# Graph attention layers: h of two graphs is read back by four DMAs in every second step, and both are split one step on

## The reference

```python
def _L0_gnn_ref(seq_inputs, Wq, bq, Wk, bk, Wv, bv, Wf, bf, graph_mask):
    q = _heads(seq_inputs @ Wq + bq)
    k = _heads(seq_inputs @ Wk + bk)
    v = _heads(seq_inputs @ Wv + bv)
    scores = jnp.einsum('bhqd,bhkd->bhqk', q, k) / np.sqrt(HEAD_SIZE)
    bias = jnp.where(graph_mask, 0.0, NEG)[:, None]
    probs = jax.nn.softmax(scores + bias, axis=-1)
    ctx = jnp.einsum('bhqk,bhkd->bhqd', probs, v)
    ...
    return ctx @ Wf + bf
h = jnp.maximum(_layernorm(x, axis=-1), 0.0)
x = x + _L0_gnn_ref(h, ..., adj)
h = jnp.maximum(_layernorm(x, axis=-1), 0.0)
x = x + _L1_gnn_ref(h, ..., adj)
```

## Time and profile before

| | us |
|---|---|
| median of 3 runs | 1942.06 |
| lowest, highest | 1934.52, 1944.56 |
| the profiled execution | 1940.74 |
| its span on the core | 1938.7 |
| TensorE busy | 1869.9 (96%) |
| VectorE busy | 1479.7 (76%) |
| ACT busy | 1526.5 (79%) |
| POOL busy | 1185.7 (61%) |

### The profile page before, as it was taken

How to read it: one execution, slowest core, us unless ns; L and a number is a source line. 1 busy time by engine, 2 the same in 40 slices (tenths; PEclk the granted TensorE clock), 3 DMA queues, 4 the chain that set the end, 5 groups by cost and what they waited for, 6 DMA issues and landing times.

```text
span 1938.7 us, 58154 instructions
## 1 busy us (share of the span) xinstructions
PE 1869.9 (96%) x15766; PEld 1079.6 (56%) x15766; DVE 1479.7 (76%) x5312; ACT 1526.5 (79%) x4553; POOL 1185.7 (61%) x1800
## 2 busy tenths in 40 slices
PE   3899999999999999999999999999999999999996
PEld 1455555555555555555555555555555555555553
DVE  5788777778777777777777787777787777877765
ACT  3688878878888777888887788888888888888874
POOL 3576666666666566666665666666666666666642
PEclk9999999999999999999999999999999999999999
DMA  6466666666666566666666666666666666655554
GB/s 185 131 188 183 199 179 193 193 189 204 202 183 189 176 190 202 191 184 198 194 205 184 182 192 193 193 199 205 188 192 198 197 204 192 198 182 179 180 168 155
DMA packets 445247, 365.35 MB, mean 188 GB/s; under 512 B 212450, under 2 KB 412132, under 8 KB 444900
## 3 DMA queue, kind: packets, MB, share of 16 engines
q1 hardware_dynamic: 444900, 361.43, 61.9%
HBM read 185.09 MB, written 176.16 MB: 186 GB/s over the span
## 4 chain that ended last, share of the span: by engine, by line
PE 50%; SPq 28%; DMA 9%; issue 8%; ACT 2%; DVE 2%; POOL 1%; POOLq 0%; DVEq 0%; ACTq 0%
SPq L332 21%; PE ps_qk L494 7%; DMA p_dram<-p_blocks 7%; PE ps_shared L494 7%; PE ps_shared L496 7%; PE ps_shared L495 7%; PE ps_qk L496 7%; PE ps_qk L495 7%; PE ps_shared L551 5%; PE ps_scores L571 4%; SPq L324 2%; ACT probs L669 1%; SPq L104 1%; SPq L293 1%; SPq L340 1%
## 5 line engine op out<-in xcount | busy, mean ns | idle before, releaser
L669 ACT ACTIVATE probs<-probs,exp_bias,exp_scale 128x128 f32<-128x128 f32 x1536 | 734.7, 482 | 13.1 <-issue 6.6
L430 POOL TENSOR_TENSOR probs<-probs,row_rcp 128x768 f32<-128x768 f32 x256 | 376.6, 1471 | 545.9 <-DVE row_rcp L831 545.9
L854 DVE CUSTOM_DVE_ANT_0 probs<-ps_scores,mask 128x128 f32<-128x128 f32 x1536 | 345.9, 287 | 40.9 <-issue 40.9
L841 DVE SCALAR_TENSOR_TENSOR qk_lo<-ps_qk,qk_bias,qk_hi 128x512 f16<-128x512 f32 x384 | 279.7, 747 | 112.7 <-ACT qk_hi L653 111.5
L648 ACT ACTIVATE v<-ps_shared 128x384 f32<-128x384 f32 x256 | 125.6, 491 | 259.4 <-PE ps_shared L496 259.3
L864 DVE SCALAR_TENSOR_TENSOR x_tile<-ps_shared,out_scale,x_tile 128x384 f32<-128x384 f32 x256 | 157.6, 616 | 195.5 <-PE ps_shared L496 195.3
L669 ACT ACTIVATION_READ_ACCUMULATOR probs<-probs,exp_bias,exp_scale 128x1 f32 x1536 | 292.2, 190 | 0.0
L653 ACT ACTIVATE qk_hi<-ps_qk,qk_bias 128x512 f16<-128x512 f32 x384 | 259.4, 676 | 38.9 <-PE ps_qk L496 38.9
L437 POOL TENSOR_TENSOR ht_lo<-h_moved,ht_hi 128x384 f16<-128x384 f32 x256 | 236.3, 923 | 53.7 <-ACT ht_hi L639 52.8
L419 POOL TENSOR_TENSOR x_tile<-x_tile,out_bias 128x384 f32<-128x384 f32 x256 | 256.6, 1003 | 0.0
L494 PE MATMUL ps_shared<-wf_hi,ct_hi 128*128 128x384 f16 x768 | 251.7, 328 | 3.8 <-DVE ct_lo L835 3.8
(11 more groups left out here) (85 smaller groups left out, 3544.1 us busy)
## 6 DMA issues: line engine op xcount, KB each, us to landing
p_dram<-p_blocks SPq DMA_DIRECT2D x256, 384.0 KB, 2.4
p_moved<-p_dram SPq DMA_DIRECT2D x1024, 96.0 KB, 2.5
h_dram<-h_blocks SPq DMA_DIRECT2D x256, 192.0 KB, 2.2
h_moved<-h_dram SPq DMA_DIRECT2D x1024, 48.0 KB, 2.0
x_tile<-in_x SPq DMA_DIRECT2D x128, 192.0 KB, 2.8
out_x<-x_tile SPq DMA_DIRECT2D x128, 192.0 KB, 2.3
adj_u<-in_adj SPq DMA_DIRECT2D x64, 64.0 KB, 2.3
wv_raw<-in_L_gnn_Wv SPq DMA_DIRECT2D x2, 576.0 KB, 4.9
```

The source lines that it names most:

```text
L430: nc.gpsimd.tensor_tensor(probs[i % 2][:, :, :], probs[i % 2][:, :, :], row_rcp[i % 2][:, :].rearrange("p (a o) -> p a o", o=1) .to_broadc ...
L669: ins = nc.scalar.activation(probs[i % 2][:, s, :], probs[i % 2][:, s, :], ACT.Exp, bias=exp_bias[i % 2][:, s:s + 1], scale=exp_scale[laye ...
L841: nc.vector.scalar_tensor_tensor(out=qk_lo[b][:, chunk, :], in0=ps_qk[chunk % QK_BANKS][:, :], scalar=qk_bias[layer_of(t)][:, chunk // KT, ...
L854: ins = nc.vector.tensor_tensor_reduce(probs[i % 2][:, s, :], score_bank(i, s // PAIRS)[:, (s % PAIRS) * P:(s % PAIRS + 1) * P], mask[b][: ...
```

## The change

`h_moved` becomes one tile that holds two graphs, side by side. SP still writes h of every graph on its own. But it reads h back only in even steps, for graphs s + 8 and s + 9 together, with four DMAs that each bring both (32 partitions x 8 pieces of 96 numbers), and these stand ahead of the step's reads of probabilities. They wait for the writes of both graphs, the later of which was issued in the same step, and until the pair before has been split. ACT and POOL split both graphs in the odd step that follows: the odd one in the step it had, the even one a step later than before. `h_back` has two semaphores instead of four. The order ahead of the first slot follows suit.

```diff
-        h_moved = [sb(f"h_moved{k}", [P, QUADS, RUN], F32) for k in range(2)]
+        h_moved = sb("h_moved", [P, 2, QUADS, RUN], F32)
...
-        h_back = [sem(f"h_back{i}") for i in range(PER)]
+        h_back = [sem(f"h_back{j}") for j in range(PER // 2)]
...
+            def keep_h(t, i, m):
+
+                wait_apart(sp, count, h_back[i // 2], unit_count(t, m, 16 * QUADS))
+                wait_apart(sp, count, h_blocked, unit_count(t, m, PER, i + 1))
+                sp.dma_start(h_dram[i, :, :, :, :].rearrange("a r b n -> (a r) b n"), h_blocks[i % 2][:, :, :]
+                             ).then_inc(h_kept[i], 16)
+
+            def bring_h(t, i, m):
+
+                wait_apart(sp, count, ht_set, unit_count(t, m, PER, i - 1))
+                for k in (i - 1, i):
+                    wait_apart(sp, count, h_kept[k], unit_count(t, m, 16, 16))
+                for quad in range(QUADS):
+                    sp.dma_start(h_moved[quad * SQ:(quad + 1) * SQ, :, :, :],
+                                 h_dram[i - 1:i + 1, :, :, quad, :].rearrange("g a r n -> r g a n")
+                                 ).then_inc(h_back[i // 2], 16)
...
+                    if exists(hu) and hi % 2:
+                        bring_h(hu, hi, m)
                     if exists(pu):
-                        bring_back(pu, pi, p_dram, p_moved, p_kept, p_back, ctx_summed, m)
-                    if exists(hu):
-                        bring_back(hu, hi, h_dram, h_moved, h_kept, h_back, ht_set, m)
+                        bring_probs(pu, pi, m)
...
-                bring_back(0, i, h_dram, h_moved, h_kept, h_back, ht_set, None)
+                keep_h(0, i, None)
+            bring_h(0, 1, None)
...
             load_weight(1, 3)
-            bring_back(1, 0, h_dram, h_moved, h_kept, h_back, ht_set, None)
             load_weight(1, 2)
...
-                    if exists(hu):
+                    if exists(hu) and hi % 2:
+                        h_lo(hu, hi - 1, m)
                         h_lo(hu, hi, m)
...
-                act.wait_ge(h_back[i], unit_count(t, m, 16 * QUADS, 16 * QUADS))
-                nc.scalar.activation(in_order(ht_hi[b][:, :, rows]), moved_in_order(h_moved[i % 2]), ACT.Copy
+                act.wait_ge(h_back[i // 2], unit_count(t, m, 16 * QUADS, 16 * QUADS))
+                nc.scalar.activation(in_order(ht_hi[b][:, :, rows]), moved_in_order(i % 2), ACT.Copy
                                      ).then_inc(ht_hi_set, 1)
...
-                    if exists(hu):
+                    if exists(hu) and hi % 2:
+                        h_hi(hu, hi - 1, m)
                         h_hi(hu, hi, m)
```

More of the change, by code:

```diff
@@ L267, in build, with moved_in_order @@
         ps_largest, ps_bias = ps_scores[2], ps_scores[3]
-        def moved_in_order(tile):
-            return tile[:, :, :].rearrange("p a (c k) -> p c a k", c=KT)
+        def moved_in_order(k):
+            return h_moved[:, k, :, :].rearrange("p a (c k) -> p c a k", c=KT)
         def in_order(view):
@@ L318, in load_out_bias @@
                 sp.dma_start(f_bias_raw[:, :], layers[l]["bf"].rearrange("(a n) -> a n", a=1)).then_inc(f_loaded, 16)
-            def keep_blocks(t, i, blocked, blocks, dram, kept, back, m):
-                wait_apart(sp, count, back[i], unit_count(t, m, 16 * QUADS))
-                wait_apart(sp, count, blocked, unit_count(t, m, PER, i + 1))
-                sp.dma_start(dram[i, :, :, :, :].rearrange("a r b n -> (a r) b n"), blocks[i % 2][:, :, :]
-                             ).then_inc(kept[i], 16)
@@ L327, in bring_back, with keep_probs @@
-            def bring_back(t, i, dram, moved, kept, back, taken, m):
-                wait_apart(sp, count, taken, unit_count(t, m, PER, i - 1))
-                wait_apart(sp, count, kept[i], unit_count(t, m, 16, 16))
-                for quad in range(QUADS):
-                    sp.dma_start(moved[i % 2][quad * SQ:(quad + 1) * SQ, :, :],
-                                 dram[i, :, :, quad, :].rearrange("a r n -> r a n")).then_inc(back[i], 16)
+            def keep_probs(t, i, m):
+                wait_apart(sp, count, p_back[i], unit_count(t, m, 16 * QUADS))
+                wait_apart(sp, count, p_blocked, unit_count(t, m, PER, i + 1))
+                sp.dma_start(p_dram[i, :, :, :, :].rearrange("a r b n -> (a r) b n"), p_blocks[i % 2][:, :, :]
+                             ).then_inc(p_kept[i], 16)
@@ new lines, in bring_probs @@
+            def bring_probs(t, i, m):
+                wait_apart(sp, count, ctx_summed, unit_count(t, m, PER, i - 1))
+                wait_apart(sp, count, p_kept[i], unit_count(t, m, 16, 16))
+                for quad in range(QUADS):
+                    sp.dma_start(p_moved[i % 2][quad * SQ:(quad + 1) * SQ, :, :],
+                                 p_dram[i, :, :, quad, :].rearrange("a r n -> r a n")).then_inc(p_back[i], 16)
+            def keep_h(t, i, m):
[3 more added lines that the diff above has]
+                             ).then_inc(h_kept[i], 16)
@@ L348, in slot @@
                     if exists(pu):
-                        keep_blocks(pu, pi, p_blocked, p_blocks, p_dram, p_kept, p_back, m)
+                        keep_probs(pu, pi, m)
                     if exists(hu):
-                        keep_blocks(hu, hi, h_blocked, h_blocks, h_dram, h_kept, h_back, m)
+                        keep_h(hu, hi, m)
                     if exists(su) and layer_of(su) == 1:
@@ L373, in _ @@
             for i in range(2):
-                keep_blocks(0, i, h_blocked, h_blocks, h_dram, h_kept, h_back, None)
-            for i in range(2):
-                bring_back(0, i, h_dram, h_moved, h_kept, h_back, ht_set, None)
+                keep_h(0, i, None)
+            bring_h(0, 1, None)
             for i in range(PER):
@@ L379, in _ @@
             for i in range(2, PER):
-                keep_blocks(0, i, h_blocked, h_blocks, h_dram, h_kept, h_back, None)
+                keep_h(0, i, None)
             load_adj(0, None)
-            for i in range(2, PER):
-                bring_back(0, i, h_dram, h_moved, h_kept, h_back, ht_set, None)
+            bring_h(0, 3, None)
             for i in range(PER):
@@ L387, in _ @@
             load_out_bias(1)
-            keep_blocks(1, 0, h_blocked, h_blocks, h_dram, h_kept, h_back, None)
+            keep_h(1, 0, None)
             load_weight(1, 3)
-            bring_back(1, 0, h_dram, h_moved, h_kept, h_back, ht_set, None)
             load_weight(1, 2)
@@ L436, in h_lo @@
                 pool.wait_ge(ht_hi_set, unit_count(t, m, PER, i + 1))
-                nc.gpsimd.tensor_tensor(in_order(ht_lo[b][:, :, rows]), moved_in_order(h_moved[i % 2]),
+                nc.gpsimd.tensor_tensor(in_order(ht_lo[b][:, :, rows]), moved_in_order(i % 2),
                                         in_order(ht_hi[b][:, :, rows]), ALU.subtract).then_inc(ht_set, 1)
```

## The result

The changed kernel took 1926.35 us (median of 14 runs, 1923.43 to 1931.14). The kernel before took 1936.82 us in 14 runs beside them (1929.59 to 1944.56). The ratio is 0.994, with a 95% interval from 0.9927 to 0.9953: 11.6 us faster, between 9 and 14. The profiled execution took 1926.46 us with a span of 1924.3, where that of before had a span of 1938.7. These two lie 14.4 us apart. The profiled execution of before stands 3.9 us above its median, that of after stands on it, so the traces show somewhat more than the median gain.

What follows compares the result with a forecast made beforehand. TensorE and SP's queue were taken to bound the kernel by turns. -13 (p_moved) - 2 (start) + 1 (ACT and VectorE) = -14 us from 1942.06 gave 1928; forecast 1918 to 1932 (0.57), range 1918 to 1943.

Steps and rivals of the forecast that it cites:

- p_moved, -13: TensorE's waits for moved probabilities in steady running: 13 us counted as won, of at most 18.7.
- SP, -2.0 for four issues in the odd step: SP's odd step loses four h reads: 1.73 us of issuing and about 0.3 us of waits.
- The pair read's issue, no addition: SP's even step: four reads of twice the bytes take no longer to issue; the other end was +1.73 us.
- The wait for h's write, +0.5 in an even step: SP's even step: h reads wait for the h write just issued, 0 to 0.5 us, taken as 0.5.
- the fourth rival: SP: issues left out give nothing back, the new wait adds 20 x 0.5 = 10 us; 1950, chance 0.02.
- The odd probabilities land 2.7 us sooner: SP, in the pair shown: next write at 716.7 instead of 719.39, odd probabilities landing 2.7 us sooner.
- Long issues leave a few waits: SP: occasional long issues leave TensorE a few waits, so 13 of the 18.7 us count as won.
- the first rival: SP: the pair read costs what two reads did, p_moved stays late; 1940 us (1934 to 1946), chance 0.25.
- ACT and VectorE, +1: Odd step: the later qk_hi delays VectorE's residual by at most 0.15 us; 1 us in all, for a few pairs.
- waits for ct_lo ahead of v in dozens: TensorE, ahead of the projection of v: a listed sign that the forecast is wrong.
- The third rival: VectorE passes ACT's 0.4 us delay on to the projection of v: +18 us, 1960, chance 0.06.
- The start, -2: First slot: TensorE's 6.39 us wait goes; between nothing and 6.4 us won, taken as 2.

Runs made afterwards that it cites:

- e_three_more_issues: The changed kernel with three small 12 KB reads more issued by SP at the end of every odd step: 1946.65 us, ratio 1.0043.
- e_splits_only: The kernel before with four buffers for h_moved and both splits of a pair in the odd step, SP's order kept: 1939.3 us, ratio 1.002.
- e_order_only: The kernel before, its eight h reads kept, with even steps' reads of h ahead of those of probabilities: 1986.56 us, ratio 1.0255.
- e_pair_behind_probs: The changed kernel with the pair of h read behind the probabilities in the even step: 1924.16 us, ratio 0.9935.
- e_eight_reads: The changed kernel with the pair of h read by eight DMAs of one graph each in the same place: 2018.5 us, ratio 1.0418.
- e_qk_before_splits: The changed kernel with ACT's two splits of an odd step behind that step's last qk_hi: 1924.11 us, ratio 0.993.

## Why the prediction was right, point by point

**The forecast** was 1928 and the measured median is 1926.35. Both its parts are a little off and cancel: the gain is 11.6 where 14 was forecast, and it was counted from the median of three runs, 1942.06, where fourteen give 1936.82. From that, the forecast's -14 would have given 1923. In the profiled executions the sum holds almost to the microsecond (-14 against -14.4).

**p_moved, -13.** Late contexts went from 17.5 to 4.35 us, that is -13.2. The ceiling of 18.7, taken from the rate of matmuls, was good for 17.5. The profiled executions show more than the medians here: the profiled run of before was in the upper half of runs that differ by 15 us, where those of the changed kernel differ by 8. The kernels nearest to the threshold, `e_three_more_issues` and `e_splits_only`, differ most, by 21 and 18 us; that the threshold is why is argued.

**SP, -2.0 for four issues in the odd step.** Confirmed by putting them back: 2.0 us of SP's time for four small reads. The sum of all issues fell by 1.8 us, gaps between them not counted. The rule of the Trainium skill that stood against it ("DMA: Bandwidth & Descriptors", "Anatomy of one DMA") has the fixed cost of a DMA in its completion and not in its setup. That section is headed for the path of GpSimd, so its 50 ns for the dispatch was no price for SP's queue, and the estimate of 0.2 us made from it could not be expected to hold. On SP's queue the setup was not small: SP stood 1.72 us for four reads of 12 KB, and with three or four of them more TensorE was the one to wait. The rule's other half, that the completion is the long part, agrees with the trace: a write of h landed 2.2 us (median) after its issue, and the wait for it alone cost 49 us in `e_order_only`.

**The pair read's issue, no addition.** 1.80 us (median) for four, where the four reads of h of an odd step took 1.74. The rival that it costs what two did, and the one that it costs half, are out. So is "h issues of over 0.6 us each". The step from eight reads to four in the same place was worth 92 us.

**The wait for h's write, +0.5 in an even step.** It measured 0.38 us in `e_order_only` and 0.29 between the two kernels with four more issues. The mechanism of the fourth rival ("the new wait outweighs the issues") is real. I priced it at 20 waits x 0.5 = 10 us, and alone it costs 49, since it puts SP over the threshold in every pair and not just in the twenty that waited already. That step of the working was wrong by a factor of five, without harm to the forecast: with the issues gone SP is under 14.36 and the wait is free, as `e_pair_behind_probs` shows.

**"The odd probabilities land 2.7 us sooner."** This step failed in size. The sum of two steps had given 1.5 us and only the pair written out gave 2.7, since its even step was taken 0.6 us shorter instead of 0.5 longer. From the landing of the odd probabilities to the start of the context that uses them there are 0.79 us now (median), and there were 0.50. Two things take the rest. SP ran into VectorE, as its late start fell from 1.80 to 1.04 us and in even steps to 0.09. And the odd step's write of probabilities lands 2.91 us after its issue (median), where it took 2.37: in flight ahead of it are now four reads of probabilities, 384 KB, directly behind the 384 KB of the pair read, where before the last ones ahead of it were 192 KB of h. The two are seen together; that the bytes are the cause is argued, not shown. Their number alone does not set it: `e_eight_reads` has the same bytes in the same order ahead of this write, and there it landed after 2.56 us. The 0.3 us sufficed all the same: contexts with at most 0.12 us to spare went from 36 to 7. The even ones gave 6.88 - 5.21 = 1.7 us of slack, where I had said 2.5.

**Long issues leave a few waits.** Issues of over 0.9 us number 98 after and 112 before, so one falls into most pairs. They moved: before, 77 of them fell on reads of h, and now 4 do, but 69 on reads of probabilities (26 before). On the pair read in this place, where the first rival wanted them, they hardly fell. I had summed SP's need for two steps to 12.9 without one and 14.1 with one. The issues put back place it at 13.0 on average, worked out from a kernel in which SP ends last. The mean between the writes of the changed kernel itself, 14.46, is TensorE's pace and says only that SP is not over it.

**ACT and VectorE, +1.** ACT behaves as said: its wait ahead of v in odd steps is 0.24 us (mean) where it was 0.62, and 0.65 in the earlier trace rows. VectorE in the changed kernel, an odd step, answers to the earlier trace rows:

```profile
712.68 1.63 DVE L857 SCALAR_TENSOR_TENSOR qk_lo<-ps_qk,qk_bias,qk_hi 128x512 f16<-128x512 f32 x2
714.23 0.97 DVE L823 STREAM_TRANSPOSE p_blocks<-probs 128x768 f32<-128x768 f32 x1
715.24 0.62 DVE L880 SCALAR_TENSOR_TENSOR x_tile<-ps_shared,out_scale,x_tile 128x384 f32<-128x384 f32 x1
```

The idle 0.27 us ahead of the residual has gone (0.05 on average), as the delay was to use it up. The projection of v starts late for 10.9 us in all, where it was 8.5: +2.4, of the order of the +1. The splits are not shown to be the cause of it, as `e_splits_only` has both in the odd step and 8.5 us, and `e_qk_before_splits` has 11.6. The sign of being wrong, "waits for ct_lo ahead of v in dozens", was badly chosen. The list of waits names 7 of them, but by the starts of the weight loads all 43 late projections are waits for it, and so were 35 in the kernel before: they were there all along, and most belong to VectorE's wait for the mask. The pair of the earlier trace rows is one of them. The third rival, 18 us slower, did not come about, and the splits alone are within 0.5% of nothing.

**POOL, 0.** It has both splits in a piece of 1.79 us and the scaling behind them waits 0.18 us for VectorE where it waited 1.07:

```profile
713.19 1.79 POOL L451 TENSOR_TENSOR ht_lo<-h_moved,ht_hi 128x384 f16<-128x384 f32 x2
...
717.48 1.47 POOL L444 TENSOR_TENSOR probs<-probs,row_rcp 128x768 f32<-128x768 f32 x1 [0.18 <-DVE row_rcp L847]
```

The cover that I named is nearly used up: another 0.2 us on POOL in this step would be seen by the scaling. In `e_qk_before_splits` nothing of it is left (0.03 us in the mean), and the kernel is not slower by it.

**h in time.** ACT starts the first split of a pair 3.4 us (median) after the reads have landed and the second 3.8; before, the two graphs had 1.1 and 0.9 us. It never waits there in steady running.

**The start, -2.** The first scores start at 63.83 instead of 65.68: -1.85. TensorE's timeline, which answers to the earlier trace rows:

```profile
47.67 0.38 PE L509 MATMUL ps_qk<-ht_hi,wk_hi 128*128 128x512 f16 x1 [2.49 <-DVE qk_lo L857]
...
63.83 0.23 PE L586 MATMUL ps_scores<-qk_hi 64*128 64x128 f16 x2 [0.30 <-DVE largest_all L772]
```

The 6.39 us are gone and two waits of 2.49 and 2.60 stand in their place, and ahead of the first scores stands VectorE's work on the weights (`largest_all`), as I had taken it.

**What limited the gain to 12 us.** The change has two parts of opposite sign. In kernels where SP ends last, the added wait is worth +36 to +49 us and the four issues fewer in two steps 69 (with the wait) or 92 (eight reads against four). The kernel before had nothing to lose but 17.5 us, as its two steps on SP (14.59 between the writes) barely exceed TensorE's 14.36. The rest of what SP gained has become idle time of SP, in front of VectorE.

## What to carry to other kernels

Before you cost a change on a queue, work out that queue's need in one period and the period of the engine it feeds. Under it an added wait or issue cost nothing that could be told from noise here, over it most of its length in every period: two more issues cost 1 to 3 us, three 20 to 22, four 69. Do not price a wait by the number of times that the profile shows the engine waiting today; count it in every period from which the sum is over. And try an order and its saving apart: here a net gain of 12 us stood over a loss of 49 from the order alone. An idle time that the profile calls "issue" may still be a wait: hold the start behind it against the ends of what it needs.

## What the hardware showed

- A read of 256 pieces of 384 bytes (96 KB) was issued in 0.45 us (median), one of 128 pieces in 0.43 and one of 32 pieces (12 KB) in 0.42. On this queue, the time of issuing reads went with the number of DMAs and hardly with their pieces.
- The odd step's write of 384 KB landed 2.37 us (median) after issue before, and 2.91 after, with more bytes of reads directly ahead of it. In the mean it was 3.09 with the pair read behind the probabilities, and 2.75 where four small reads were added to that at the end of the odd step, which is not directly ahead of this write. With eight reads in place of the pair's four it was 2.56 (median). What sets it is open.
- An issue of over 0.9 us comes in most stretches of two steps: 98 in the changed kernel, 112 before, 78 to 117 in the others. All 98 (111 of the 112 before) have a packet of the queues that the page calls instruction within the 1.5 us ahead of them or during them; of the issues of up to 0.5 us, 21% have (20% before). Whether these packets cause them was not tried.
- A projection of v that waits for a `ct_lo` begins 0.115 us behind its end, and the view calls such a wait "issue". In the nine kernels with a median of up to 1947 us there are 32 to 44 of these waits (8.1 to 11.8 us), and in the four slower ones, in which SP holds TensorE up, 2 to 21 (1.1 to 5.1 us).
- One more wait in VectorE's queue, for a mask that ACT had made at least 12.5 us before, took 0.2 us: the gap ahead of the maxima is 0.38 us with it and 0.17 without.
